# Feed-forward tiles of 256 and of 128 rows in place of tiles of 256 alone

## What is computed

```python
def xattn(x, latents, ...):                       # heads 16, dim_head 64
    x, lat = layer_norm(x), layer_norm(latents)
    q = lat @ Wq
    k, v = split(concat([x, lat], axis=1) @ Wkv)
    attn = softmax(q k^T * scale)
    return (attn v) @ Wout
def ffn(x, gate_w, w1, b1, w2, b2):               # 3584 tokens of 256 numbers
    scores, idx = top_k(softmax(x @ gate_w), 2);  scores /= sum(scores)
    h = gelu(x @ w1[e] + b1[e])                   # 256 -> 1024, each expert e
    y = h @ w2[e] + b2[e]                         # 1024 -> 256
    return sum over the two chosen experts of score * y
x = x + tanh(g_xattn) * xattn(ctx, layernorm(x), ...)
x = x + tanh(g_ffn) * ffn(layernorm(x), ...)
```

## Time and profile before

| | |
|---|---|
| median of 3 runs | 1821.69 us (1819.88 to 1821.77) |
| profiled execution | 1821.99 us, its span 1820.3 us |
| TensorE matmul busy | 1663.3 us, 91% of the span |
| VectorE busy | 1316.1 us, 72% |
| ScalarE busy | 1199.0 us, 66% |
| GpSimd busy | 1255.9 us, 69% |
| first matmul of the tiles, last y finished | 1404.3 us, 1797.8 us |
| copy to the output issued | 1806.7 us |

### The profile page before, as it was taken

How to read it: one execution, slowest core, us unless ns; L and a number is a source line. 1 busy time by engine, 2 the same in 40 slices (tenths; PEclk the granted TensorE clock), 3 DMA queues, 4 the chain that set the end, 5 groups by cost and what they waited for, 6 DMA issues and landing times. The chain is left out here.

```text
span 1820.3 us, 42338 instructions
## 1 busy us (share of the span) xinstructions
PE 1663.3 (91%) x15046; PEld 1165.6 (64%) x15046; DVE 1316.1 (72%) x3073; ACT 1199.0 (66%) x2733; POOL 1255.9 (69%) x1350
## 2 busy tenths in 40 slices
PE   1899999999999999999999999999952999999995
PEld 0456666666666666666666666655642889999994
DVE  4677787777878777787777777787644876666662
ACT  2587777777877777787777777777753654444442
POOL 5387777777778888887888878886674344555442
PEclk9999999999999999999999999999975999999998
DMA  4167776676667678676766766655777432233334
GB/s 148 35 139 137 149 148 137 144 154 138 145 133 148 138 145 152 137 141 132 144 135 148 143 132 136 132 101 103 167 145 225 134 59 48 48 51 52 53 48 105
DMA packets 597544, 223.37 MB, mean 123 GB/s; under 512 B 535202, under 2 KB 587984, under 8 KB 596892
## 3 DMA queue, kind: packets, MB, share of 16 engines
q1 hardware_dynamic: 581804, 202.18, 52.8%
q0 software_dynamic: 15536, 18.49, 6.6%
HBM read 71.39 MB, written 20.76 MB: 51 GB/s over the span
## 5 line engine op out<-in xcount | busy, mean ns | idle before, releaser
L532 POOL TENSOR_TENSOR p_parts<-p_space,p_parts 112x487 f16<-112x487 f32 x512 | 559.3, 1115 | 141.2 <-ACT p_parts L669 140.2
L660 ACT ACTIVATE p_space<-scores_ps,shift 112x487 f32<-112x487 f32 x508 | 335.2, 664 | 8.9 <-POOL p_parts L532 4.4
L715 ACT ACTIVATE k_hi<-proj_ps 128x488 fp32r<-128x488 f32 x256 | 148.0, 578 | 265.9 <-PE proj_ps L1129 265.8
L885 DVE TENSOR_SCALAR_CACHE_REDUCE passed<-scores_ps 112x487 f16<-112x487 f32 x502 | 302.3, 659 | 24.6 <-PE scores_ps L1153 24.5
L669 ACT ACTIVATE p_parts<-p_space 112x487 f16<-112x487 f32 x512 | 276.3, 607 | 0.0
L960 DVE SCALAR_TENSOR_TENSOR v_sb<-proj_ps,v_sb 128x512 f16<-128x512 f32 (+1 forms) x256 | 176.6, 690 | 136.7 <-ACT v_sb L729 130.0
L765 ACT ACTIVATE o_space<-scores_ps,b_sb,undo 128x256 f32<-128x256 f32 x280 | 139.4, 559 | 195.2 <-PE scores_ps L1283 191.4
L636 POOL DMA_INDIRECT sums_dram<-pt_space,ot_space x70 | 117.7, 1682 | 191.9 <-ACT pt_space L775 178.2
L954 DVE TENSOR_TENSOR k_lo<-proj_ps,k_hi 128x488 fp32r<-128x488 f32 x256 | 169.3, 661 | 93.4 <-ACT k_hi L715 92.9
L1184 PE MATMUL pv_ps<-v_sb,pt_space 128*128 128x128 f16 x2048 | 218.0, 221 | 7.9 <-DVE o_space L1006 6.0
L1129 PE MATMUL proj_ps<-kv_hi,wkv_hi 128*128 128x488 f16 x512 | 191.5, 374 | 36.7 <-POOL kv_lo L559 13.5
(11 more groups left out here) (232 smaller groups left out, 3563.1 us busy)
## 6 DMA issues: line engine op xcount, KB each, us to landing
w_part<-in_L_ffn_w_dram SPq DMA_DIRECT2D x64, 256.0 KB
arena<-in_L_ffn_w_dram SPq DMA_DIRECT2D x28, 512.0 KB
ctx_sb<-in_ctx_dram SPq DMA_DIRECT2D x32, 375.0 KB
pt_space<-p_parts SPq DMA_TRANSPOSE x256, 4.0
x_sb<-in_x_dram SPq DMA_DIRECT2D x32, 112.0 KB
res_sb<-in_x_dram SPq DMA_DIRECT2D x32, 112.0 KB
sums_dram<-x_sb SPq DMA_DIRECT2D x32, 112.0 KB, 2.8
xn_dram<-xn_sb SPq DMA_DIRECT2D x32, 112.0 KB, 2.1
```

The source lines that it names most:

```text
L532: pool.tensor_tensor(p_parts[0:LQ, p % PS, h, 1, 0:LK], p_f[0:LQ, p % 2, h, 0:LK], p_parts[0:LQ, p % PS, h, 0, 0:LK], ALU.subtract).then_i ...
L660: act.activation(p_f[0:LQ, p % 2, h, 0:LK], score_bank(p, h)[0:LQ, 0:LK], ACT.Exp, bias=shift[0:LQ, p // 2 % 2, n:n + 1], scale=-1.0, accu ...
L715: act.activation(k_hi[:, j], ps[:, 0:LKP], ACT.Copy).then_inc(kq_high, 1)
L885: dve.tensor_scalar(passed_of(p, h), score_bank(p, h)[0:LQ, 0:LK], P_SHIFT, None, ALU.add, ALU.min, accum_out=shift[0:LQ, p // 2 % 2, n:n ...
```

## The change

The tile loop gets 28 tiles of 256 rows ("pair") and 10 of 128 ("single"): `ORDER` has eight pairs first, then ten times two pairs and a single. There are 38 tiles and 66 halves. In a single, each operation of the loop has half the columns or half the instructions: h has 48 matmuls of 128 columns in place of 256, the transposes are 2 in place of 4, y has 24 matmuls in place of 48, and there are one gather, one weighing and one add in place of two.

Each expert's count of rows is rounded up to 128. An expert gets count // 256 pairs (of the count so rounded), and its odd block goes to a single, or to a pair that `least_end` adds. The slot computation takes 21 VectorE instructions in place of nine, and `tile_expert` is filled by two copies in place of one. Six GpSimd instructions prepare its constants at the program's start, in place of one.

`least_end` guarantees less than before: tile n may belong to an expert up to n+2 (`AHEAD` is 2). So the h of tile n waits, for n+2 below 8, for 4(n+3) units, and the turns at which the units are split are moved earlier.

```diff
-TILES = (TOKENS * TOPK + E * (ROWS - 1)) // ROWS
-HALVES = 2 * TILES
+PAIR_TILES, SINGLE_TILES = 28, 10
+TILES = PAIR_TILES + SINGLE_TILES
+HALVES = 2 * PAIR_TILES + SINGLE_TILES
+AHEAD = 2
+ORDER = [("pair", n) for n in range(PAIR_TILES - 2 * SINGLE_TILES)]
+for n in range(SINGLE_TILES):
+    first = PAIR_TILES - 2 * SINGLE_TILES + 2 * n
+    ORDER += [("pair", first), ("pair", first + 1), ("single", n)]
...
-TILE_SPLITS = {-2: (14,), -1: (15, 16), 0: (17, 18, 19), 1: (20, 21, 22), 2: (23, 24, 25), 3: (26, 27, 28), 4: (29, 30), 5: (31,)}
+TILE_SPLITS = {-2: (14, 15), -1: (16, 17), 0: (18, 19, 20), 1: (21, 22, 23), 2: (24, 25, 26, 27), 3: (28, 29, 30, 31)}
...
-                for a in range(2):
-                    n = 2 * t + a
+                for a, n in enumerate(halves_of(t)):
                     pool.indirect_dma_start(xs_sb[:, t % 2, a], None, xn_rows, bass.IndirectOffsetOnAxis(ap=token_row[:, n:n + 1], axis=0)).then_inc(x_read[t % 2], 16)
...
+                wide = 2 * rows_of(t)
+                g_hi, g_lo = g_parts[:, s, 0, m, 0:wide], g_parts[:, s, 1, m, 0:wide]
...
-                    if n < E:
-                        pe.wait_ge(unit_low, 4 * (n + 1))
+                    rows = rows_of(n)
+                    if n + AHEAD < E:
+                        pe.wait_ge(unit_low, 4 * (n + AHEAD + 1))
...
-                                    last = nc.tensor.matmul(h_ps[m][:, c * ROWS:c * ROWS + ROWS], experts[:, bass.ds(e1, 1), at:at + 128].rearrange("p o f -> p (o f)"),
-                                                            (xt_hi, xt_lo)[x_][:, n % 2, k], start=(k == i == 0), stop=(k == KD - 1 and i == 2))
+                                    last = nc.tensor.matmul(h_ps[m][:, c * rows:c * rows + rows], experts[:, bass.ds(e1, 1), at:at + 128].rearrange("p o f -> p (o f)"),
+                                                            (xt_hi, xt_lo)[x_][:, n % 2, k, 0:rows], start=(k == i == 0), stop=(k == KD - 1 and i == 2))
...
-                    for r in range(2):
+                    rows = rows_of(t)
+                    for r in range(rows // HALF):
```

More of the change, by code:

```diff
@@ L27, with halves_of, rows_of, moved_of @@
 ROWS = 256
-TILES = (TOKENS * TOPK + E * (ROWS - 1)) // ROWS
-HALVES = 2 * TILES
-EXPERT_HALVES = TOKENS // 128
-TABLE_ROWS = 252
+HALF = 128
+PAIR_TILES, SINGLE_TILES = 28, 10
+TILES = PAIR_TILES + SINGLE_TILES
+HALVES = 2 * PAIR_TILES + SINGLE_TILES
+SEGMENTS = 2 * E
+EXPERT_HALVES = TOKENS // HALF
+TABLE_ROWS = 252
+AHEAD = 2
[3 more added lines that the diff above has]
+    ORDER += [("pair", first), ("pair", first + 1), ("single", n)]
+def halves_of(t):
+    kind, n = ORDER[t]
+    return (2 * n, 2 * n + 1) if kind == "pair" else (2 * PAIR_TILES + n,)
+def rows_of(t):
+    return HALF * len(halves_of(t))
+def moved_of(t):
+    return 16 * sum(len(halves_of(u)) for u in range(t % 2, t + 1, 2))
+def expert_index(t):
+    kind, n = ORDER[t]
+    return n if kind == "pair" else PAIR_TILES + n
 X_SCALE = 1024.0
@@ L260, in program @@
         spare_fill = x2_sb
[L261 to L266, removed]
+        least_end = sb("least_end", [128, E])
+        list_row = sb("list_row", [128, E])
+        expert_step = sb("expert_step", [128, SEGMENTS])
+        reached = sb("reached", [128, 2, SEGMENTS])
+        spare_words = picked[:, :, :, :].rearrange("p n k e -> p (n k e)")
+        count_i = spare_words[:, 0:E].bitcast(I32)
+        blocks_i = spare_words[:, E:2 * E].bitcast(I32)
+        pairs_i = spare_words[:, 2 * E:3 * E].bitcast(I32)
+        pairs_f = spare_words[:, 3 * E:4 * E]
+        left = spare_words[:, 4 * E:5 * E]
+        pair_end = spare_words[:, 40:41 + E]
+        own_pairs = spare_words[:, 49:49 + E]
+        single = spare_words[:, 57:58 + E]
+        single_row = spare_words[:, 66:66 + E]
+        ends = spare_words[:, 74:74 + SEGMENTS]
+        offset = spare_words[:, 90:91 + SEGMENTS]
+        offset_step = spare_words[:, 107:107 + SEGMENTS]
         found = sb("found", [128, 2])
@@ L1051, in _ @@
[L1051 to L1054, removed]
+            dve.memset(pair_end[HS, 0:1], 0.0)
@@ new lines, in _ @@
+            dve.scalar_tensor_tensor(out=single_row[HS, :], in0=own_pairs[HS, :], scalar=2.0, in1=list_row[HS, :], op0=ALU.mult, op1=ALU.add)
+            s_then(dve.tensor_tensor(single[HS, 1:], left[HS, :], own_pairs[HS, :], ALU.is_gt))
+            s_then(dve.tensor_tensor_scan(ends[HS, E - 1:], ones[HS, 0:E + 1], single[HS, :], 0.0, ALU.mult, ALU.add))
+            dve.scalar_tensor_tensor(out=reached[HS, 1], in0=ends[HS, :], scalar=row_no[HS, 0:1], in1=expert_step[HS, :], op0=ALU.is_le, op1=ALU.mult)
@@ L1287, in _ @@
                     n = t + 2
-                    pe.wait_ge(x_read[n % 2], (n // 2 + 1) * 32)
+                    rows = rows_of(n)
+                    pe.wait_ge(x_read[n % 2], moved_of(n))
                     if n >= 1:
@@ L1291, in _ @@
                     for k in range(KD):
-                        for a in range(2):
-                            last = nc.tensor.transpose(xt_ps[:, k * ROWS + a * 128:k * ROWS + a * 128 + 128], xs_sb[:, n % 2, a, k * 128:k * 128 + 128], ident[:, :])
+                        for a in range(len(halves_of(n))):
+                            last = nc.tensor.transpose(xt_ps[:, k * rows + a * 128:k * rows + a * 128 + 128], xs_sb[:, n % 2, a, k * 128:k * 128 + 128], ident[:, :])
                     last.then_inc(xt_done, 1)
```

73 lines of the change are left out of this document (46 added, 27 removed).

## The result

| | before | after |
|---|---|---|
| median | 1821.73 us (4 runs) | 1842.13 us (4 runs, 1840.75 to 1846.51) |
| ratio | | 1.0114, 95% interval 1.0096 to 1.0131 |
| profiled execution | 1821.99, span 1820.3 | 1841.04, span 1839.3 |
| first matmul of the tiles | 1404.3 | 1406.3 |
| end of the last y but one | 1792.6 | 1813.5 |

A forecast was written before the change was run, and what follows sets the result against it. From the first feed-forward tile the kernel was taken as bound by TensorE, 10.92 us a tile. Terms -18.6 - 1.9 - 4.0 + 23.2 + 9.2 + 9.0 + 4.3 = +21.2 gave 1843 us, range 1832 to 1853.

The forecast's parts named there:

- Matmuls saved: Tile loop on TensorE: fewer rows save 21.2 us, of which 2.6 fall behind the last y but one: -18.6 us.
- waits of before gone: TensorE's existing waits among the h of tiles 2 to 7 go, last weights being required by tile 5: -4.0 us.
- the end: Kernel's end: the last tile has one add in place of two, which start 1.86 apart: -1.9 us.
- Waits for weights: Before h of tiles 2 to 5, TensorE waits for VectorE's splits, 3.7, 4.9, 6.1 and 8.5 us: +23.2 us.
- The clock: TensorE's granted clock halves after each of four new gaps, 2.3 us each: +9.2 us, bounds 4.5 and 12.
- Small tiles: 128-row tiles: address instructions delay y 0.9 us, ten times, +9.0; next h waits 0.48 for VectorE's copy, nine times, +4.3.
- Slot computation: Ahead of the tiles: about 3.2 us in place of 1.7, hidden behind the table's gather held by the entries: 0.
- (a): Rival, tiles 2 to 5: VectorE has the units split when TensorE asks, no gaps or clock cost; 1811, chance 0.04.
- (b): Rival, small tiles: small h runs at the array's pace, sequencer's lead covering it, +9.0 goes; 1834, chance 0.08.
- (d): Rival, small h: weight loads of 98 ns bind, 4.7 us in place of 3.0, ten times 1.7; 1860, chance 0.07.
- (c): Rival, new gaps: the clock stays at full through them, as after the 2.5 us one; 1834, chance 0.08.

The follow-up runs named there:

- early_splits: Changed kernel, AHEAD still 2, with the weight units split in earlier turns (12 to 15 ahead of the tiles): 1815.25 us, ratio 0.9963.
- fixed_weights: Changed kernel with h of the ten small tiles taking expert 0's weights at a fixed address, without address instructions: 1829.77 us in a single execution.
- large_one_read: Kernel before, 35 tiles of 256 rows, with TensorE reading the expert's number once a tile: 1821.26 us, ratio 0.9994.
- filled_gaps: Changed kernel with 38, 48 and 72 extra unused matmuls ahead of the waits of tiles 3, 4 and 5: 1839.37 us, ratio 1.0093.
- waits_only: Kernel before with only the change's new waits and split turns, all tiles at 256 rows, old slot computation: 1848.05 us, ratio 1.0141.
- one_read: Changed kernel with TensorE reading each tile's expert number once, ahead of h, and keeping it for y: 1838.88 us, ratio 1.0089.
- copy_first: Changed kernel with VectorE copying the next tile's transposes ahead of the Gelu m=2 split in nine small-y turns: 1841.77 us, ratio 1.011.
- slots_long: Kernel before with eight more waited instructions of 0.2 us in the slot computation: 1822.56 us, ratio 1.0002.
- ahead0: Changed kernel with AHEAD 0, waits for 4(n+1) units and the split turns of the kernel before: 1815.73 us, ratio 0.9964.

## Why the prediction was right

By its steps, in the profiled executions:

- **Matmuls saved, -18.6; waits of before gone, -4.0; the end, -1.9.** The last y but one ends 20.85 us later than before, the span is 19.0 longer: the end gives 1.85 back. No wait stands before the h of tiles 6 and 7.
- **Waits for weights, +23.2.** The chain has gaps of 3.5, 4.6, 5.8 and 8.5 us, in all 22.4 (22.5 in the table of waits). The forecast had 3.7, 4.9, 6.1 and 8.5, but counted each from the place where the next matmul would have started, which is 0.17 us earlier than the end in the chain. Counted in its way the four are 23.1. The split of unit 31 came as worked out, its load 3.8 us where 3.5 stood in the sum. The kernel with the waits alone shows that this is the deciding term.
- **The clock, +9.2.** 5.6. This is the term that was mis-sized most: after the first gap the clock stayed at full, and the other three cost 1.4, 2.5 and 1.7. The sum lies in the forecast's bounds (4.5 to 12), the cheapest gap a little under the 1.5 of its lower one, and four times the middle was too high. The kernel with the waits alone paid 7.8 for the same gaps, so the term is not one number.
- **Small tiles, +9.0 and +4.3.** 28.77 a group of three against 27.36 by columns is 1.41, where 0.9 and 0.48 make 1.38. Measured it is 0.90 between h and y, 0.41 after the small y, and 0.1 in the large y behind the gap, which the forecast had not. From the h of tile 9 to the last y it comes to 13.7: 281.2 us, where columns alone need 267.5. The two parts were told apart by single edits. The claim on which the first rests, that the address instructions and not the array set the pace, was shown by taking them away.
- **Slot computation, 0.** table_row was written at 1386.96, for 1387.2 forecast, and that the row numbers themselves come early enough was right: the gather was issued at 1388.74, 0.25 us later than before. But it took 7.95 us to land in place of 6.90, and the first y began 0.8 later. The forecast saw that the two splits behind the slot computation come later, and looked for harm in their loads; what they did was lengthen the gather's issue by 0.70 us. The other 0.35 of the later landing stays open. In the changed kernel no wait downstream takes the 0.8 up. Over all profiles the landing takes 6.9 to 7.6 us in four with the old slots and 7.8 to 11.3 in eight with the new ones. The first y starts at 1423.5 and 1425.4 in the mean, but there the kinds overlap, and two of the eight have more splits in that place, so the mean is no price of the new slots.

Measured terms: -18.6 - 4.0 + 23.1 + 5.6 + 13.7 - 1.9 + 0.8 = +18.7, against +19.0 in the profiles; 0.3 us are unexplained. The mechanism was right, and the closeness of the total is in part luck: the clock was 3.6 too dear, while the later start and some of the small tiles' loss, 1.2 together, were missing. The medians lie 20.4 us apart and the profiles 19.0, so agreement to 1 us says little of the terms by itself.

Of the rivals, (a), the covered wait, is what early_splits makes true, and its time there is 1815; the forecast gave 1811, with the small tiles' 13.3 us in it and 4.0 us of removed waits of which 0.65 came back, and the first y starts 4.2 us later in that profile than in the changed kernel's. (b) and (d) are refuted by fixed_weights: the array and the loads could have done it, the sequencer could not. (c) held for the first gap alone, and its one row, the full clock after the gap of 2.5 us, was thin: in large_one_read a gap of 2.2 us at the same place was followed by a slow h (7.08).

The Trainium skill's figure of about 81 ns for a matmul of 128 columns in a stream ("TensorE: Matmul & The Clock Gate", section "Back-to-back issue gap") is not what limits here: with a fixed address the small h ran at 56 ns with its weight loads, with the address instructions at 63 (3.0 us for 48), after a lead of 1.2 us.

## What to carry to other kernels

Before a rule on which work needs which data is loosened, count when that data is ready and who makes it: here the looser bound, n+2 in place of n, put 13 splits in TensorE's way (2, 3, 4 and 4 in the four gaps), and a table of turns was worth more than all matmuls that the new tiles saved. When an engine's work is moved in time, look also at what then runs beside it: the splits that came later here slowed GpSimd's issue of a gather on which the whole stage waits. Halving a matmul's columns halves its time only while the sequencer keeps up; look at the address and register instructions between the matmuls, since behind long matmuls they are free and behind short ones they are the bound. Judge a small remedy on the version whose large waits are gone, since beside them its gain may not reach the median.

## What the runs showed of the hardware

- TensorE's sequencer needs about 129 ns for an address instruction with the one or two matmuls behind it (4.0 us from the first to the last of 32), and about 0.8 us from the read of a number in SBUF to the first address instruction that uses it (1491.4 to 1492.2). Neither shows as busy time.
- A gather whose issue on GpSimd ran beside VectorE's weight splits (128x1024, 1.2 us each) was held until they ended: the issue took 0.99 us with none beside it, 1.69 with 0.82 us of them and 5.34 with 4.47.
- The same gap of 3.5 us on TensorE was followed by a full clock in three profiles (h 5.41 or 5.42: the changed kernel, filled_gaps, fixed_weights) and by a slow one in three (7.08: waits_only, one_read, copy_first). In the three with a full clock the h of tile 1 had run 7.08 or 7.09 us, in the other three 5.43, 6.81 and 5.41; whether that decides is not shown. A gap of 2.2 us, too, came out both ways (5.41 in slots_long and ahead0, 7.08 in large_one_read). Gaps of 4.6 us and more were followed by a slow h in all of the five profiles that have them unfilled, and cost 1.4 to 2.8 us each. With matmuls of no use in the gap the clock stayed at full.
- Matmuls of 128 columns with a weight load each ran at 56 ns over a whole h (2.68 us for 48, fixed_weights).
